# A second convolution placed ahead of image 0's transposes, with its pixels fetched in four quarters

## What is computed

```
patches = im.reshape(b, c, hp, P, wp, P)
x = jnp.einsum('bchpwq,dcpq->bhwd', patches, conv_w)
x = x.reshape(b, hp * wp, -1) + conv_b
for i in range(2):
    y = _ln(x, ln1_g[i], ln1_b[i])
    q, k, v = jnp.split(y @ qkv_w[i], 3, axis=-1)
    ...
    x = x + att @ out_w[i] + out_b[i]
    y = _ln(x, ln2_g[i], ln2_b[i])
    x = x + gelu(y @ ff1_w[i] + ff1_b[i]) @ ff2_w[i] + ff2_b[i]
```

## Time and profile before

| | us |
|---|---|
| median of 3 runs | 754.61 |
| lowest, highest | 753.69, 755.52 |
| the profiled execution | 752.73 |
| its span, first to last instruction | 751.0 |
| PE busy in it | 657.5 (88%) |
| DVE, ACT, POOL busy | 435.3, 386.0, 345.8 |
| mean granted clock of TensorE | 0.944 |

### The profile page before, as it was taken

One profiled execution on the slowest core, in us unless ns is written; L12 is line 12 of the kernel. 1 busy time (PEld: TensorE's weight loads), 2 busy tenths in 40 slices (PEclk: granted clock), 3 DMA queues, 4 the chain that ended last, 5 costly groups with the idle time before them and its releaser, 6 DMA issues.

```text
span 751.0 us, 17613 instructions
## 1 busy us (share of the span) xinstructions
PE 657.5 (88%) x5070; PEld 434.1 (58%) x5071; DVE 435.3 (58%) x1478; ACT 386.0 (51%) x721; POOL 345.8 (46%) x401
## 2 busy tenths in 40 slices
PE   4888899888875999999999999549999999999980
PEld 4776786578642222222222222338999999999970
DVE  0346757775674277777777764436655666566640
ACT  0323338342322899999999998014444444444430
POOL 3111333223231135555555544416777776777771
PEclk9999999999995999999999999569999999999995
DMA  8999999200013990000000000169888988888934
GB/s 333 397 343 339 322 328 340 80 1 1 22 52 118 382 311 32 30 30 30 30 30 30 32 32 31 41 202 295 228 230 230 233 229 229 229 233 229 228 58 74
DMA packets 46063, 124.74 MB, mean 166 GB/s; under 512 B 5243, under 2 KB 31292, under 8 KB 44748
## 3 DMA queue, kind: packets, MB, share of 16 engines
q1 hardware_dynamic: 32780, 108.92, 45.0%
q0 software_dynamic: 11696, 14.19, 9.4%
q10 hardware_dynamic: 1552, 1.18, 0.5%
HBM read 105.53 MB, written 58.42 MB: 218 GB/s over the span
## 4 chain that ended last, share of the span: by engine, by line
PE 71%; DVE 10%; POOL 4%; ACT 4%; DMA 4%; issue 3%; SPq 1%; ACTq 0%; DVEq 0%; POOLq 0%
PE ps L839 14%; PE ps L976 11%; PE ps L826 9%; PE ps L993 9%; PE ps L981 7%; PE ps L680 3%; ACT mid L1080 2%; POOL rstd L467 2%; DMA out<-mid 2%; DVE stat L1165 2%; DVE mid L1173 2%; PE ps L756 1%; PE ps L766 1%; PE ps L653 1%; ACT big L1042 1%
## 5 line engine op out<-in xcount | busy, mean ns | idle before, releaser
L1080 ACT ACTIVATE mid<-ps 128x1536 f32<-128x1536 f32 x144 | 200.3, 1457 | 30.0 <-PE ps L826 30.0
L839 PE MATMUL ps<-mid 128*32 128x384 f32 x1152 | 123.9, 502 | 1.3
L1507 DVE TENSOR_SCALAR mid<-ps,big 128x128 f32<-128x128 f32 x189 | 54.7, 345 | 94.2 <-PE ps L981 56.1
L976 PE MATMUL ps<-mid,big 128*128 128x128 f32 x756 | 96.1, 277 | 0.3 <-ACT mid L1106 0.3
L590 POOL TENSOR_TENSOR mid<-mid 128x384 f32<-128x384 f32 x63 | 62.9, 998 | 70.5 <-DVE mid L1516 47.8
L826 PE MATMUL ps<-mid 52*128 52x512 f16 x432 | 88.3, 390 | 5.5 <-ACT mid L1080 4.9
L976 PEld LDWEIGHTS ps<-mid,big 128*128 128x128 f32 x756 | 90.7, 194 | 0.6 <-ACT mid L1106 0.6
L993 PE MATMUL ps<-big,mid 128*128 x378 | 78.0, 343 | 1.6 <-POOL mid L590 1.5
L1113 ACT ACTIVATE mid<-mid 128x384 f32<-128x384 f32 x63 | 33.0, 523 | 73.3 <-DVE mid L1507 73.3
L541 POOL DMA_INDIRECT expert_in<-big,slot_u x48 | 48.0, 1000 | 46.4 <-DVE slot_u L1398 35.5
L993 PEld LDWEIGHTS ps<-big,mid 128*128 128x128 f32 x378 | 59.7, 189 | 9.3 <-issue 2.1
(11 more groups left out here) (224 smaller groups left out, 1103.3 us busy)
## 6 DMA issues: line engine op xcount, KB each, us to landing
big<-w_cat SPq DMA_DIRECT2D x63, 576.0 KB, 3.9
expert_in<-expert_in SPq DMA_DIRECT2D x16, 1774.5 KB, 46.2
big<-expert_in SPq DMA_DIRECT2D x63, 136.5 KB, 3.5
big<-patches SPq DMA_DIRECT2D x3, 2048.0 KB, 21.2
w_cat<-w_a SPq DMA_DIRECT2D x1, 6144.0 KB, 32.8
big<-w SPq DMA_DIRECT2D x1, 4608.0 KB, 14.7
w_cat<-w_b SPq DMA_DIRECT2D x2, 1536.0 KB, 30.0
big<-patches SPq DMA_DIRECT2D x4, 512.0 KB, 7.6
```

The source lines that it names most:

```text
L839: last = nc.tensor.matmul(oacc[32 * g:32 * g + 32, 0:QW], vhead[par][:, kb, :], probs[kb % 3][:, g * QW:(g + 1) * QW], start=(kb == 0), st ...
L976: nc.tensor.matmul(banks[half][:, c * P:(c + 1) * P], w1_t[q][:, half * FF + c * P:half * FF + (c + 1) * P], xtT[r][:, 0:P], start=(c == 0 ...
L1080: nc.scalar.activation(probs[kb % 3], SETS[kb % 2], ACT.Exp, scale=0.5).then_inc(probs_ready, 1)
L1507: last = nc.vector.tensor_scalar(glu[r][:, c * P:(c + 1) * P], bank(1 + r)[:, c * P:(c + 1) * P], b1_cols[:, bass.ds(ex * 6 + c, 1)], 7.0, ...
```

## The change

The second and the third entry of the order change places, so that conv of image 1 stands directly behind conv of image 0, ahead of T of image 0. On DVE nothing moves by this, as T has no part there. On PE conv 1 passes T0; on POOL the norm of image 1 passes T0's bias addition; on ACT conv has no part. Conv 1 takes the form of conv 0: both tiles at each slice, with a wait for each quarter of the pixels. The pixels of image 1 are fetched in four transfers of 512 KB in place of one of 2048 KB, directly behind `rows`, so ahead of `cols`, which they stood behind before.

```diff
-    return [(*lane[slot - start], b, tiles) for slot in range(len(LANE) + NB - 1)
-            for start, lane, b, tiles in lanes if 0 <= slot - start < len(lane)]
+    order = [(*lane[slot - start], b, tiles) for slot in range(len(LANE) + NB - 1)
+             for start, lane, b, tiles in lanes if 0 <= slot - start < len(lane)]
+    order[1:3] = [order[2], order[1]]
+    return order
...
-        convw_in, patch0_in = [[sem(f"{name}{q}") for q in range(4)] for name in ("convw_in", "patch0_in")]
-        patch_in = [None] + [sem(f"patch_in{b}") for b in range(1, NB)]
+        convw_in, patch0_in, patch1_in = [[sem(f"{name}{q}") for q in range(4)] for name in ("convw_in", "patch0_in", "patch1_in")]
+        patch_in = [None, None] + [sem(f"patch_in{b}") for b in range(2, NB)]
...
-            for dst, src, s in ((rows_sb, rows[:, 0:5 * D].broadcast_to([P, 5 * D]), rows_in), (cols_sb[:], cols, cols_in),
-                                (patch_sb[1], patches[1], patch_in[1]), (qkvw_sb, qkv_w, qkvw_in),
+            sp.dma_start(rows_sb, rows[:, 0:5 * D].broadcast_to([P, 5 * D])).then_inc(rows_in, 16)
+            for k in range(0, KT, KT // 4):
+                ks = slice(k, k + KT // 4)
+                sp.dma_start(patch_sb[1][:, ks, :], patches[1][:, ks, :]).then_inc(patch1_in[k * 4 // KT], 16)
+            for dst, src, s in ((cols_sb[:], cols, cols_in), (qkvw_sb, qkv_w, qkvw_in),
...
-                if stage == "conv" and b == 0:
+                if stage == "conv" and b < 2:
...
-                            pe.wait_ge(patch0_in[k * 4 // KT], 16)
+                            pe.wait_ge((patch0_in, patch1_in)[b][k * 4 // KT], 16)
...
-                if stage == "conv" and b:
+                if stage == "conv" and b >= 2:
```

## The result

| | before | after |
|---|---|---|
| median of 20 runs, us | 753.82 | 751.11 |
| lowest to highest | 752.42 to 755.78 | 748.14 to 755.63 |
| ratio, 95% interval | | 0.9961 [0.9948, 0.9974] |
| the profiled execution, and its span | 752.73, 751.0 | 750.02, 748.2 |

The changed kernel is faster by 0.39%, 2.9 us with an interval from 2.0 to 3.9. The forecast was 1.8 us, just outside that interval. The order of events came out as forecast, to within 0.2 us; the size is larger than the sum, and most of what follows is about that rest.

What follows compares the result with a forecast made beforehand. PE, busy 88% of the span, was taken as the bound, with waits of 3.26 and 1.06 us before image 0's and image 1's transposes. 754.61 - 1.8 (image 1's transposes 1.79 us earlier) = 752.8 us; range 750.8 to 754.9.

Steps and rivals of the forecast that it cites:

- Conv 1 forward: Second convolution on PE starts at 17.04 us, once both banks are free; pixel quarters land about 15.3 to 19.1, costing no wait.
- Length of conv 1: Second convolution with both pixel halves alternating between two banks: takes 7.15 us, the alternation costing nothing, and ends at 24.19.
- T0 at 24.19 and the new wait: Image 0's transposes start at 24.19; ACT's table load and copy then make 2.52 us to image 0's projections, some 2.1 idle.
- The last rival: Rival about ACT's table switch, putting 1.4 us on top of the load before image 0's projections; chance 0.02.
- T1 at 31.87 with PE as the bound: Image 1's transposes start at 31.87 us instead of 33.66, straight after image 0's projections, with PE waiting for nobody.
- POOL's moved addition: Bias addition now on POOL beside DVE's last step of image 1's norm: delay unknown, bounded at 0 to 0.7 us.
- The thread's term: Image 1's transposes move from 33.66 to 31.87 us: 1.79 us gained, of which 1.06 is the wait before them.
- From conv 2 on the thread is shifted, not changed, to the end: From the third convolution on, every queue keeps its order, so the gain of 1.79 us carries unchanged to the end.
- a fall less: Rival: later waits meet TensorE's clock elsewhere, or a fall behind the 3.26 us wait goes; 1.5 us less, 751.3; chance 0.20.
- A0 at half clock: Rival: the new 2.1 us wait brings a clock fall, image 0's projections end 1.5 us later, 754.3; chance 0.17.
- The profile's distance of 1.88 us under the median: Profiled execution of the kernel before, 752.73 us, lies 1.88 us under the median of three runs, 754.61.
- the slower rival: Clock falls ahead of image 0's projections and stays down some 9 us, losing 4.5 us: 757.3; chance 0.05.

Runs made afterwards that it cites:

- experiment 1: Only the new order, image 1's pixels still one transfer of 2048 KB, against the kernel before: ratio 0.9991, median 756.43 us.
- experiment 2: Only the pixel quarters and the two-bank form, second convolution still behind image 0's transposes, against the kernel before: ratio 0.9996.
- 4: Changed kernel plus one 128x1 activation at the start of ACT's list, so its table load is done early: ratio 0.9929 to the kernel before.
- 8: Kernel before plus one 128x1 activation at the start of ACT's list, so its table load is done early: ratio 1.0002 to the kernel before.
- 9: Changed kernel plus 8 useless matmuls (1.8 us) on PE between image 1's transposes and the third convolution: ratio 0.9996 to the kernel before.
- 3: Kernel before plus 13 useless matmuls on PE in the 3.26 us wait ahead of image 0's transposes: ratio 0.9994 to the kernel before.
- 11: Changed kernel plus 11 useless matmuls on PE in the wait ahead of image 2's transposes: ratio 0.9946 to the kernel before.
- 6: Changed kernel plus 8 useless matmuls (1.8 us) on PE in the new wait ahead of image 0's projections: ratio 0.9949 to the kernel before.

## Why the prediction was right, and what in it was not

- Conv 1 forward: 17.04 forecast, 17.11 came. Landings of 15.3 and 19.1 forecast for the first and the last quarter; 15.4 and 19.2 came. Without them nothing is won (experiment 1).
- Length of conv 1 in the form with two banks: 7.15, came 7.23, and 7.16 in experiment 2.
- T0 at 24.19 and the new wait: 24.34, and 2.47 us to A0 against 2.52. A0 at 26.71: 26.81. That the table load is 1.28 us of it was shown by taking it away (4) and by its costing nothing before (8). The last rival, at 0.02, puts 1.4 us on top of the load, and no run shows this term: early loading shortened T0 to A0 by 1.34 us, 1.28 of them the load itself, and in both traces, before and after, ACT starts the load 0.08 us behind T0's last matmul and the copy 0.02 us behind the load.
- T1 at 31.87 with PE as the bound: 32.04, without a wait. The unknown cost of POOL's moved addition, 0 to 0.73, is 0.4 us on DVE, and nobody waits for it. The thread's term, 1.79 us, measured 1.62 between the two traces, and 1.65 counted from the end of conv 0.
- "From conv 2 on the thread is shifted, not changed, to the end": this is what the sum had wrong. The shift was kept until T2 (1.66 us) and then grew to 3.2 us behind conv 3, by a fall of the clock less. The term mis-sized is the clock's: the sum puts it at nothing, and it measured about 1.5 us at conv 3 in both traces of the change. I had this as a rival, "a fall less", at 0.20. Its 1.5 us are 0.50 of the 3.0 us from 49 us and 0.43 of the 3.3 us from 62 us; at conv 3 the lead grew by 1.53 us (1.69 to 3.22). Of its two reasons, the first, that the waits behind the change meet the clock elsewhere, agrees with the traces, whose falls come at other times (59 and 179 us in the change, 49, 62 and 182 before), and 9 supports it; the second, falls behind the 3.26 us wait in other executions, was not found (3), though the times don't exclude it.
- The median of 751.11 lies near that rival's 751.3 in part by luck. The forecast of 752.8 starts from 754.61, the median of three runs, and that of 20 is 753.82: 0.8 of the 1.7 us between forecast and result are this base, and only some 1 us is the change's larger effect.
- The clock's row also shows a low stretch in the slices from 469 to 507 us, which the prediction counts among the short ones. The change doesn't touch it: the clock reads 0.50 from 472.5 to 502.5 us in before and from 469 to 499 us in the change.
- "A0 at half clock" exists: in the traces of 1 and 11, at 1.7 us, against 1.5 estimated. It came in two of the five traces that have this wait, not in those of the change.
- The profile's distance of 1.88 us under the median shrank with more runs: the median of 20 is 753.82, so 1.1 us.

Of the slower rival, a long fall ahead of A0, no trace shows anything: each fall up to 200 us was over within 4 us. A longer low stretch that begins between 220 and 229 us is in every trace, in most of them with some us of full clock in it.

## What to carry to other kernels

Work that is moved to fill a wait uncovers what it covered: 3.26 us of wait were filled, a table load of 1.28 us and the copy behind it came out, and 1.6 us stayed, so look for the partner edit (here one tiny activation early) that is worth nothing before and 0.9 us on the thread after. An order and the transfers that feed it are one change: either half alone gave nothing that could be measured. And behind a shift of 1.6 us the falls of TensorE's clock came at other times and were one fewer in both traces of the change, which was worth about as much as the edit itself, 1.5 us; such a size needs many runs, not one trace, and here even 20 runs of each bound it only to 2.0 to 3.9 us for both together.

## What the runs showed that was not expected

A fall of the clock that is prevented can come back: with the 2.62 us wait filled in the kernel before, the trace has none of the falls at 49, 62 and 182 us but others at 89, 134 and 165, which took back the 2.7 us that PE was ahead by 70 us, and the time stayed (1.0008). It is one trace, and what made the later falls is not shown. And ACT's load of 1.28 us in the shadow of another engine is free to within 0.04 us (8). With the same code the first convolution took from 8.8 to 9.9 us in these traces, its slow beginning being longer or shorter: PE starts 5 matmuls in a us at first and 9 later, and the step comes near 10.5 us in 1 and 6 and near 12.5 us in 9. The first pace is near that of a fall, but the granted clock reads 1.00 all through it, so what makes this beginning slow is not shown.
